# One fp32 product in place of three split products for the q/k projection of a 96-step attention stage

## What is computed

```python
def attn_layer(x, Wqkv, qs, ksc, Wo):          # x: 16 sequences x 256 x 128
    q, k, v = jnp.split(x @ Wqkv, 3, -1)        # 16 heads of 64; Wqkv 128 x 3072
    q = l2norm(q) * qs;  k = l2norm(k) * ksc
    q = q * cos * scale + rotate_half(q) * sin * scale
    k = k * cos / scale + rotate_half(k) * sin / scale
    return local_attention(q, k, v) @ Wo        # windows of 32, one look back

for layer in range(6):                          # x is layer-normed once before the stack
    x = x + attn_layer(shift_tokens(x), ...)
    x = x + ffn_layer(shift_tokens(x), ...)     # layernorm, 128 -> 2 x 341 -> 128, gelu gate
```

## Time and profile before

| what | value |
|---|---|
| time, median of 3 runs | 6092.23 us (6086.14 to 6094.33) |
| span of the profiled execution | 6084.7 us |
| PE busy | 82% of the span |
| DVE busy | 76% |
| ACT busy | 61% |
| POOL busy | 38% |
| DMA engines busy | 1.9% |
| mean granted clock of TensorE | 0.929 |

### The profile page before, as it was taken

One profiled execution on the slowest core, in us unless ns is written; L12 is line 12 of the kernel. 1 busy time (PEld: TensorE's weight loads), 2 busy tenths in 40 slices (PEclk: granted clock), 3 DMA queues, 4 the chain that ended last, 5 costly groups with the idle time before them and its releaser, 6 DMA issues.

```text
span 6084.7 us, 134581 instructions
## 1 busy us (share of the span) xinstructions
PE 5008.3 (82%) x48122; PEld 3287.9 (54%) x48122; DVE 4647.8 (76%) x7187; ACT 3688.6 (61%) x6807; POOL 2332.8 (38%) x1142
## 2 busy tenths in 40 slices
PE   2369999999588888888888888888888888888886
PEld 1124488888455555555555455555555555555554
DVE  7751255555788888888888888888888888888887
ACT  3333355555466666666666666666666666666665
POOL 1000000000354555554554555554555554554554
PEclk7679999999799999999999999999999999999998
DMA  1000000000100000000000000000000000000001
GB/s 55 0 0 0 18 1 0 0 0 0 36 0 0 0 0 10 8 0 0 0 18 0 0 0 0 18 0 0 0 0 18 0 0 0 0 18 0 0 0 31
DMA packets 43315, 34.87 MB, mean 6 GB/s; under 512 B 3771, under 2 KB 39062, under 8 KB 42262
## 3 DMA queue, kind: packets, MB, share of 16 engines
q1 hardware_dynamic: 43286, 34.52, 1.9%
HBM read 30.32 MB, written 4.19 MB: 6 GB/s over the span
## 4 chain that ended last, share of the span: by engine, by line
PE 38%; DVE 34%; issue 17%; DVEq 3%; ACT 2%; POOL 0%; DMA 0%; ACTq 0%; SPq 0%; POOLq 0%
DVE arena L925 7%; PE bank L1449 5%; DVE arena L947 5%; PE bank L1359 5%; PE bank L800 4%; PE bank L764 4%; PE bank L532 4%; PE bank L1385 3%; DVE arena L967 3%; DVE arena L149 3%; DVE arena L953 3%; DVE arena L959 2%; PE bank L1407 2%; PE bank L751 2%; PE bank L755 2%
## 5 line engine op out<-in xcount | busy, mean ns | idle before, releaser
L1301 POOL TENSOR_TENSOR arena<-arena,rope_d 128x512 f32<-128x512 f32 x780 | 1288.2, 1681 | 1083.9 <-DVE arena L935 1083.9
L1407 PE MATMUL bank<-m_vo,arena 128*32 128x512 f32 x6144 | 867.3, 689 | 374.2 <-ACT arena L1185 371.5
L1307 POOL TENSOR_TENSOR arena<-arena 128x2048 f32<-128x2048 f32 x195 | 898.4, 4607 | 590.4 <-DVE arena L947 573.3
L947 DVE TENSOR_TENSOR arena<-arena,rope_d 128x1024 f32<-128x1024 f32 x390 | 715.5, 1854 | 13.9
L1135 ACT ACTIVATE arena<-bank 128x512 f32<-128x512 f32 x784 | 468.5, 598 | 389.0 <-PE bank L1359 359.7
L1359 PE MATMUL bank<-wqk_split,x_split 128*128 (+1 forms) x2352 | 680.2, 425 | 15.3 <-ACT arena L1135 10.4
L1407 PEld LDWEIGHTS bank<-m_vo,arena 128*32 128x32 f32 x6144 | 172.8, 117 | 870.4 <-ACT arena L1185 705.7
L1369 PE MATMUL bank<-ident,arena 128*128 128x128 f32 x3104 | 435.8, 284 | 103.8 <-ACT arena L1156 100.0
L1359 PEld LDWEIGHTS bank<-wqk_split,x_split 128*128 128x128 f32 x2352 | 438.7, 193 | 136.7 <-issue 19.7
L1283 POOL TENSOR_TENSOR rope_d<-rope,qk_scale 128x128 f32 (+1 forms) x14 | 6.5, 463 | 1228.7 <-DVE x_all L1031 1228.7
L925 DVE TENSOR_REDUCE arena<-arena 128x16 f32<-128x1024 f32 x390 | 455.4, 1209 | 7.7 <-ACT arena L1142 7.7
(11 more groups left out here) (224 smaller groups left out, 9656.2 us busy)
## 6 DMA issues: line engine op xcount, KB each, us to landing
wqk_stage<-in_wqk SPq DMA_DIRECT2D x8, 1024.0 KB, 6.8
out_x<-x_all SPq DMA_DIRECT2D x8, 512.0 KB, 5.2
wvt<-in_wvt SPq DMA_DIRECT2D x7, 512.0 KB, 3.9
wo<-in_wo SPq DMA_DIRECT2D x7, 512.0 KB, 5.1
w<-in_w SPq DMA_DIRECT2D x7, 341.0 KB
arena<-in_wbh SPq DMA_DIRECT2D x1, 2048.0 KB, 9.9
arena<-out_x SPq DMA_DIRECT2D x4, 512.0 KB, 5.8
w<-in_w SPq DMA_DIRECT2D x7, 128.0 KB
```

Source lines behind the costliest of these rows:

```text
L947: nc.vector.tensor_tensor(d_rot[j][:, m * H:(m + 1) * H, :], d_raw[j][:, m * H:(m + 1) * H, :], tab, ALU.mult)\
L1301: last = nc.gpsimd.tensor_tensor(d_t2[:, m * H:(m + 1) * H, a:a + half], d_raw[j][:, m * H:(m + 1) * H, z:z + half], rope_d[:, bass.ds(par ...
L1307: nc.gpsimd.tensor_tensor(d_rot[j], d_rot[j], d_t2, ALU.add).then_inc(s_rope, 1)
L1407: last = nc.tensor.matmul(bank[6 + w % 2][q * WIN:(q + 1) * WIN, :], d_xv[:, w * WIN:(w + 1) * WIN], m_vo[:, 4 * q:4 * q + 4, :].rearrange ...
```

## The change

The three products of each chunk become one plain fp32 product of unsplit tokens (`x_proj`) and unsplit weights (`wqk`). The split of the tokens becomes one copy. The split of the weights goes, and with it one link of DVE's chain; the DMA writes each layer's weights straight into one of two slots, and PE waits for the load instead of the split. SP's loop is unrolled by two so that each load has a fixed slot; a load waits until PE has projected all sequences of the layer that used the slot (`s_proj`).

```diff
-        wqk_stage = sb("wqk_stage", [P, 2 * INNER])
-        wqk_split = sb("wqk_split", [P, 2, 2, 2 * INNER], F32R)
-        x_split = sb("x_split", [P, 2, T], F32R)
+        wqk = sb("wqk", [P, 2, 2 * INNER])
+        x_proj = sb("x_proj", [P, T])
...
-        def front_split(dve, f, link):
+        def front_copy(dve, f):
...
             at_least(dve, s_proj, 8 * f)
-            link(nc.vector.tensor_copy(x_split[:, 0, :], d_xt))
-            nc.vector.tensor_tensor(x_split[:, 1, :], d_xt, x_split[:, 0, :].bitcast(F32), ALU.subtract)\
-                .then_inc(s_split, 1)
+            nc.vector.tensor_copy(x_proj[:, :], d_xt).then_inc(s_split, 1)
...
-        def split_weights(dve, layer_next, link):
...
-            dve.wait_ge(loaded_qk, 16 * (layer_next + 1))
...
-            link(nc.vector.tensor_copy(hi, wqk_stage[:, :]))
-            nc.vector.tensor_tensor(lo, wqk_stage[:, :], hi.bitcast(F32), ALU.subtract).then_inc(s_wsplit, 1)
...
-                split_weights(dve, layer + 1, link)
...
                 pe.wait_ge(s_split, f + 1)
-                pe.wait_ge(s_wsplit, layer_of(f) + 1)
+                pe.wait_ge(loaded_qk, 16 * (layer_of(f) + 1))
                 for c in chunks:
                     at_least(pe, s_raw, 4 * i + c - 1)
...
-                    for q, (xp, wp) in enumerate(((0, 0), (1, 0), (0, 1))):
-                        w = wqk_split[:, bass.ds(par, 1), wp, c * 512:(c + 1) * 512].rearrange("p a n -> p (a n)")
-                        last = nc.tensor.matmul(bank[c % 2][:, :], x_split[:, xp, j * P:(j + 1) * P], w,
-                                                start=(q == 0), stop=(q == 2))
+                    w = wqk[:, bass.ds(par, 1), c * 512:(c + 1) * 512].rearrange("p a n -> p (a n)")
+                    last = nc.tensor.matmul(bank[c % 2][:, :], x_proj[:, j * P:(j + 1) * P], w, start=True, stop=True)
                     last.then_inc(s_proj, 1)
...
-        def load_qk(sp, layer):
-            at_least(sp, s_wsplit, layer)
-            sp.dma_start(wqk_stage[:, :], weights_of("wqk", layer)).then_inc(loaded_qk, 16)
+        def load_qk(sp, layer, slot):
+            if not isinstance(layer, int):
+                sp.wait_ge(s_proj, 8 * SEQS * (layer - 1))
+            sp.dma_start(wqk[:, slot, :], weights_of("wqk", layer)).then_inc(loaded_qk, 16)
...
-            with sp.Fori(0, LAYERS) as layer:
-                load_vo(sp, layer + 1)
-                load_qk(sp, layer + 2)
-                load_ff(sp, layer + 1)
+            with sp.Fori(0, LAYERS // 2) as two:
+                for slot in range(2):
+                    layer = two * 2 + slot
+                    load_vo(sp, layer + 1)
+                    load_qk(sp, layer + 2, slot)
+                    load_ff(sp, layer + 1)
```

More of the change, by code:

```diff
@@ L18 @@
 F32 = mybir.dt.float32
-F32R = mybir.dt.float32r
 BF16 = mybir.dt.bfloat16
@@ L144, in build @@
         const_ready = sem("const_ready")
-        mask_stage = wqk_stage[:, 0:TPS * 2 * WIN].rearrange("p (t k) -> p t k", t=TPS)
+        mask_stage = wqk[:, 0, 0:TPS * 2 * WIN].rearrange("p (t k) -> p t k", t=TPS)
         def rsqrt_step(link, v, y, w):
@@ L850, in build @@
         SLOTS, SLOTS0 = 14, 10
-        (s_xs, s_split, s_ss, s_y, s_norm, s_t1, s_rope, s_tab, s_wsplit, s_proj, s_raw, s_sq, s_tp, s_tev,
+        (s_xs, s_split, s_ss, s_y, s_norm, s_t1, s_rope, s_tab, s_proj, s_raw, s_sq, s_tp, s_tev,
          s_s, s_sub, s_exp, s_prob, s_xv, s_u, s_uev, s_acc, s_x2, s_mean, s_xsq, s_varp, s_var, s_ln, s_y2, s_xn, s_up, s_gl, s_h,
@@ L855, in build @@
             sem("d_" + s) for s in (
-                "xs split ss rsq norm t1 rope tab wsplit proj raw sq tp tev s sub exp prob xv u uev acc x2 mean xsq varp "
+                "xs split ss rsq norm t1 rope tab proj raw sq tp tev s sub exp prob xv u uev acc x2 mean xsq varp "
                 "var ln rsq2 xn up gl h ffo x_done m m_ready zero chain pool_chain act_chain "
@@ L969, in softmax_prob @@
             nc.vector.tensor_tensor(d_e[j], d_e[j], d_inv.unsqueeze(1).unsqueeze(3).to_broadcast([P, 2, H, WIN]), ALU.mult).then_inc(s_prob, 1)
-        def split_weights(dve, layer_next, link):
-            par = layer_next & 1
-            dve.wait_ge(loaded_qk, 16 * (layer_next + 1))
-            hi = wqk_split[:, bass.ds(par, 1), 0, :].rearrange("p a n -> p (a n)")
-            lo = wqk_split[:, bass.ds(par, 1), 1, :].rearrange("p a n -> p (a n)")
-            link(nc.vector.tensor_copy(hi, wqk_stage[:, :]))
-            nc.vector.tensor_tensor(lo, wqk_stage[:, :], hi.bitcast(F32), ALU.subtract).then_inc(s_wsplit, 1)
         def residual(dve, n, j):
@@ L1025, in ffn_loaded @@
             return ((n + SEQS - 1) >> 4) * (16 * LOADS_FF) + 1
-        D_LINKS = 20
+        D_LINKS = 19
         def phase_d_vector(dve):
@@ L1037, in phase_d_vector @@
             link = Chain(dve, d_chain, 0, 0)
-            split_weights(dve, 0, link)
             for t in range(NT):
@@ L1053, in phase_d_vector @@
             front_tokens(dve, 0)
-            front_split(dve, 0, link)
+            front_copy(dve, 0)
             dve.wait_ge(loaded_ff, 16 * LOADS_FF + 1)
@@ L1060, in phase_d_vector @@
             front_tokens(dve, 1)
-            front_split(dve, 1, link)
+            front_copy(dve, 1)
             softmax_max(dve, 0, 0, link)
@@ L1068, in phase_d_vector @@
             with dve.Fori(0, LAYERS) as layer:
-                link = Chain(dve, d_chain, 1 + SEQS * D_LINKS, layer)
-                link.base = link.base + before
-                split_weights(dve, layer + 1, link)
                 with dve.Fori(0, SEQS) as b:
@@ L1074, in phase_d_vector @@
                     link = Chain(dve, d_chain, D_LINKS, n)
-                    link.base = link.base + (layer + 1 + before)
+                    link.base = link.base + before
                     softmax_max(dve, n, 1, link)
@@ L1085, in phase_d_vector @@
                     ffn_norm(dve, n, link, ffn_loaded(n))
-                    front_split(dve, n + 2, link)
+                    front_copy(dve, n + 2)
                     residual(dve, n, 1)
@@ L1101, in phase_d_vector @@
             link = Chain(dve, d_chain, 0, 0)
-            link.base = before + LAYERS + (LAST + 1) * D_LINKS
+            link.base = before + (LAST + 1) * D_LINKS
             ffn_centre(dve, LAST + 1, link)
@@ L1567, in _ @@
             sp.wait_ge(c_m, 4)
-            load_qk(sp, 0)
+            load_qk(sp, 0, 0)
             load_vo(sp, 0)
@@ L1574, in _ @@
                 sp.dma_start(out[s].rearrange("n p c -> p n c"), x_all[:, s, :]).then_inc(kept, 16)
-            load_qk(sp, 1)
-            with sp.Fori(0, LAYERS) as layer:
-                load_vo(sp, layer + 1)
-                load_qk(sp, layer + 2)
-                load_ff(sp, layer + 1)
+            load_qk(sp, 1, 1)
+            with sp.Fori(0, LAYERS // 2) as two:
[4 more added lines that the diff above has]
+                    load_ff(sp, layer + 1)
             sp.wait_ge(loaded_x, 16)
```

## The result

The changed kernel takes 6161.97 us (median of 4 runs, 6159.37 to 6164.66), the kernel before 6093.04 us in the same comparison: a ratio of 1.0116, 95% interval 1.0102 to 1.0131. It is slower by 69 us; 64 were forecast. The span of the profiled execution went from 6084.7 to 6157.6 us.

What follows compares the result with a forecast made beforehand. The bound was taken to be a chain hopping between engines, not one engine's sum of work. Terms: 64.3 + 0 + 0 + 0 - 5.2 + 5 = +64 us, giving 6156 us; range +35 to +80 us, 6120 to 6188, chance 0.60.

Steps and rivals of the forecast that it cites:

- PE, the loop: Projection pairs for tokens 0 to 127: 1.72 us instead of 1.38, two on the chain per iteration, +64.3 us.
- Cover over the late pairs: Pairs for tokens 128 to 255 grow 0.67 us, inside a 3.71 us wait before the last token products: cost 0.
- DVE, the loop: Dropping L918 saves 0.43 us per sequence but only lengthens DVE's idle time: gain 0, at most 41 us.
- The start of a layer: Dropped weight split at five later layer starts: gain 0, since DVE would wait for ACT's exponential; at most 17 us.
- The prologue: Serial start: splits off the chain -9.2 us, projections at low clock +4.0 us, net -5.2 us.
- SP and DMA: Weight load waits until PE has projected the layer using its slot, yet comes long before need: cost 0.
- The clock: Long iterations, slowed by a fallen clock in the up product, rise from 21 to 24 of 96: +5 us.
- rival C: Busier PE keeps 2.4 GHz, speeding the up product and the stretch around L1407: -24 us, 6068 us; chance 0.04.
- A: Clock follows badly: every second iteration becomes long, +45 us instead of +5: 6196 us, or 6185; chance 0.15.
- B: Layer starts give back 3.5 us each and half the clock loss returns: 6117 us, 6110 to 6130; chance 0.14.
- D: DVE is the bound: PE's growth is hidden, DVE's 41 us and the splits' 17 + 9 count: 6025 us; chance 0.03.
- E: No change to be seen, a mixture of C and the layer starts; chance 0.04.

Runs made afterwards that it cites:

- experiment 10: Kernel before with one fp32 product per chunk for tokens 0 to 127 alone (rounded parts), plus 5 constant products before the up product: 6117.21 us, ratio 1.0049.
- experiment 1: Kernel before with one fp32 product per chunk for tokens 128 to 255 alone, rounded parts only: 6091.0 us, ratio 1.0007.
- experiment 9: Kernel before with fp32 products for tokens 128 to 255 alone (rounded parts), plus 5 constant products before the up product: 6047.67 us, ratio 0.9932.
- experiment 3: Kernel before with DVE's part alone: no low part of tokens in the loop, weights split once, PE's three products kept: 6089.26 us, ratio 1.0007.
- experiment 8: Kernel before with PE's part alone: one fp32 product per chunk for all tokens, rounded parts, DVE still splitting: 6169.23 us, ratio 1.0134.
- experiment 6: Changed kernel plus 5 constant products ahead of the up product: 6103.72 us, ratio 1.0022 to the kernel before.
- experiment 2: Kernel before with one fp32 product per chunk for tokens 0 to 127 alone, rounded parts only: 6144.27 us, ratio 1.0098.
- experiment 4: Kernel before plus constant products on PE, 12 before the last two token products and 5 before the up product: 6068.67 us, ratio 0.9974.

## Why the prediction was right, step by step

**PE, the loop: right.** Forecast 1.72 us a pair, +0.67 us an iteration, 64.3 us. Measured 1.72 us and +0.66 in the median iteration; experiment 10 gives +66 us for this step, 54 of them away from layer starts. The Trainium skill, "FP8 and Floating Point Precision", section TensorE Precision Notes, has four passes for true fp32, and by an estimate from passes alone a pair would have taken 1.84 us: the chain shows 1.72, and the measurement decides.

**Cover over the late pairs: right.** The wait of 3.71 us shrank to 3.07 us (medians over 90 iterations of either kernel's trace), and experiments 1 and 9 show no cost.

**DVE, the loop: right.** Price 0. Experiment 3 took the work away and gained nothing; after the change the longer wait before L997 stands in its place. The copy L915 costs what the cast cost, a median of 0.286 us (changed kernel, duration ns min/median/max):

```profile
L915 DVE COPY x_proj<-arena x98: 284/286/912, 1584.7 to 6094.9; 128x256 f32<-128x256 f32 x98
```

**The start of a layer: right.** Price 0, with 3.5 us each as the most to gain. The changed kernel's timeline at a layer's start, beside the earlier trace rows:

```profile
3141.96 2.18 DVE L925 TENSOR_SCALAR arena<-arena 128x32 f32<-128x32 f32 x1
...
3146.51 1.09 ACT L1154 ACTIVATE arena<-arena 128x1024 f32<-128x1024 f32 x1
...
3147.64 1.22 DVE L963 TENSOR_REDUCE arena<-arena 128x16 f32<-128x1024 f32 x1 [3.50 <-ACT arena L1154]
```

DVE is through with L925 at 3144.14 and waits 3.50 us for ACT's exponential, which nothing in the change made earlier. The prediction had ACT later by 0.67 us there because of the longer late projections; experiment 3 has the same wait without them. The rest of the 5.4 us of the split went into L925 itself: it ran beside GpSimd's sum L1290 and took 2.18 us, where the old L929 took 0.28 us at this place, after that sum had ended.

**The prologue: right in sum, one piece off.** Forecast -5.2 us; the first L979 starts 5.2 us earlier than the first L992. DVE's side was 9.2 forecast and 9.0 measured, PE's side 4.0 forecast and 3.8 measured (experiment 8). On PE's side the pieces stood differently on the chain:

```profile
1585.09 6.29 PE bank L1341 x8
...
1597.67 3.41 PE bank L1341 x4
...
1626.04 1.96 PE bank L1341 x4
...
1640.19 3.78 PE bank L1341 x4
```

6.29 us instead of 6.88, another pair newly on the chain, and one pair of sequence 1 off it. That the pieces moved and the sum did not is chance as much as working.

**SP and DMA: right.** No wait of DVE or PE on a load appears among the waits; the page of the changed kernel has 4.8 us in the middle from issue to landing of a 1024 KB load of `wqk`.

**The clock: right in kind, too small in size.** This is the mis-sized term: +5 us for three more long iterations was taken; 9 to 11 came, 15 to 18 us. It makes up the difference between forecast and result: in the span, 0.66 x 96 = 63, -5 and +15 give 73, which is what the two spans differ by (72.9). That the term exists is shown by experiment 6. Why the count rises is shown in part. The length of an iteration alone doesn't fix it, since experiments 2 and 8 have the same short iteration (45.71 and 45.69 us) and 14 and 31 long ones. Nor do the late projections alone, with the shorter wait before the last token products that goes with them: experiment 1 has them and 20 long iterations. Only with both halves longer does the count rise. So the two were not independent, and the prediction's remark against rival C, "the change shortens only the first wait", leaves out that the second one, before the up product, doesn't stay as it was. That wait, before and after (summed over 1680 to 6030 us: us in total, times, longest):

```profile
PE bank L1449 <- DVE arena L1004: 126.0, 96, 1.8
```

```profile
PE bank L1430 <- DVE arena L991: 142.2, 93, 1.8
```

Counted over the 90 iterations from the traces, PE is idle for more than 1.45 us before the up product in 39 before and in 69 after, in 47, 29 and 70 with experiments 1, 2 and 8. Every long iteration is among these, and in each kernel about half of them are long (21, 32, 20, 14, 31). So what rose is how often PE comes early to this wait. What sets that from one iteration to the next, and why only half of these are long, stays open.

**Rivals.** A (clock follows badly) was right in sign and took a third of its price. B, C and D are out: layer starts gave nothing, the clock did not stay up by itself, DVE's work was not the bound. E is out by the interval, 1.0102 to 1.0131. C's pricing of the stretch around L1407 was wrong as well: experiment 4 gave the token products their full clock and the short iteration got 0.05 us shorter, not 0.5.

**The version that beats both.** The split kernel with five constant products ahead of the up product, 6051.24 us, ratio 0.9939 (0.9922 to 0.9955). It leaves nothing out.

## What to carry to other kernels

Three cheap products can be better than one dear one: count the pace of each from the chain, not the instructions, and look where in the iteration they stand. The same 0.66 us an iteration cost 66 us in one place and nothing in the other. Work taken from an engine is a gain only where that engine is what the next one waits for; before you count it, ask which other result the same instruction needs and when that comes. And where PE waits for another engine in every iteration, look at the granted clock behind the wait, for it can be worth more than the change under study.

## What the runs showed of the hardware

- Five 128x512 bf16 products of constants in the idle time of PE before the up product (1.3 us on average over 90 iterations) took away every long iteration (21 of 90 to none), and the kernel got 0.6% faster. Transposes stood just before that idle time in the kernel before, and the clock had fallen behind it in those 21.
- At 2.4 GHz a float32r product of 512 columns took 0.23 us on the chain with its weight load beside it, an fp32 one 0.86 us in two records.
- Eight fp32 records of 256 columns took 1.97 us at the high and 3.63 to 3.65 us where the clock had fallen.
- GpSimd's copy of 128x256 (L1317) took 2.24 us when it began beside a DVE operation with two inputs in SBUF (L935, experiment 4) and ended 0.6 us after it; it took 0.73 at the least in the same run. DVE's copy L909 behind it took 0.82 instead of 0.285 us. At a layer start L925, 32 elements, took 2.18 us beside GpSimd's sum L1290 and ended 0.04 us after it. The Trainium skill, "SBUF — State Buffer", section Who interferes with whom, calls the port pair that DVE and GpSimd share an exclusive lock, for which a DVE instruction with two inputs in SBUF contends as well. The trace agrees: GpSimd's copy was held up at L935, and DVE's L925 at L1290.
